# Adding and subtracting the context's halves on GpSimd instead of VectorE in a three-phase decoder kernel

## What is computed

```python
x  = _layernorm(x + attn(x))         # phase A: gated, decaying moments of sines and cosines
x  = _layernorm(x + xattn(x, ctx))   # phase B: autocorrelation attention against the context
x  = _layernorm(x + ffn(x))          # phase C: two branches of 8 experts with a running mean

# in phase B: FFT correlation of query and key along the 256 tokens
Qf = jnp.fft.rfft(Q, axis=2); Kf = jnp.fft.rfft(K, axis=2)
corr = jnp.fft.irfft(Qf * jnp.conj(Kf), n=Lloc, axis=2)
w, idx = jax.lax.top_k(corr.mean(axis=-1), top_k)      # top_k = 5
```

## Time and profile before

| | |
|---|---|
| median of 3 runs | 893.53 us (892.78 to 893.91) |
| the profiled execution: its time | 892.9 us |
| its span, first to last instruction | 891.1 us |
| TensorE busy | 823.9 us (92%) |
| VectorE busy | 754.2 us (85%) |
| ScalarE busy | 488.0 us (55%) |
| GpSimd busy | 98.0 us (11%) |
| TensorE's mean granted clock | 0.973 |

### The profile page before, as it was taken

The page is one execution under the profiler, slowest core; times in us unless marked ns, Lnnn a source line. Parts: engine busy times, 40 slices in busy tenths (PEclk is TensorE's granted clock), DMA queues, the critical chain, the costliest instruction groups (busy, mean ns, idle before and its releaser), DMA issues.

```text
span 891.1 us, 11684 instructions
## 1 busy us (share of the span) xinstructions
PE 823.9 (92%) x4040; PEld 489.4 (55%) x4040; DVE 754.2 (85%) x1351; ACT 488.0 (55%) x774; POOL 98.0 (11%) x164
## 2 busy tenths in 40 slices
PE   6886738999999999999999999999999999997996
PEld 3343515564755566565666475555656475656453
DVE  7987998899989998899989999899999996384133
ACT  4964763774558553866377545955395655202300
POOL 2021012000120012001120012001200022001000
PEclk9998968999999999999999999999999999999899
DMA  9475035232634343153622562234515251410040
GB/s 299 126 141 118 0 72 119 72 83 48 131 59 137 86 86 61 25 142 71 118 64 68 130 119 53 55 83 95 107 26 128 59 109 23 95 24 1 1 118 24
DMA packets 45968, 75.18 MB, mean 84 GB/s; under 512 B 4819, under 2 KB 28630, under 8 KB 45910
## 3 DMA queue, kind: packets, MB, share of 16 engines
q1 hardware_dynamic: 38998, 49.27, 22.3%
q0 software_dynamic: 6912, 25.17, 14.4%
HBM read 19.90 MB, written 4.19 MB: 27 GB/s over the span
## 4 chain that ended last, share of the span: by engine, by line
PE 48%; DVE 30%; DMA 8%; issue 8%; ACT 4%; SPq 1%; POOL 1%; ACTq 0%; DVEq 0%; POOLq 0%
DVE sc L2528 7%; PE ps L902 7%; DMA acc<-sq 7%; PE ps L911 7%; PE ps L867 6%; PE ps L785 5%; DVE sc L2520 4%; PE ps L709 4%; PE ps L751 3%; PE ps L927 3%; PE ps L726 3%; PE ps L769 2%; DVE zc L2458 2%; PE ps L844 2%; DVE frac L2500 2%
## 5 line engine op out<-in xcount | busy, mean ns | idle before, releaser
L2528 DVE TENSOR_TENSOR_SCAN sc<-mask,sc 128x1024 f32<-128x1024 bf16 x64 | 144.3, 2276 | 0.1
L911 PE MATMUL ps<-x2t,mv 128*128 128x512 f32 x256 | 119.0, 597 | 0.2
L902 PE MATMUL ps<-cum,mw 128*128 128x512 f32 x256 | 117.8, 596 | 0.6 <-DVE prod L2748 0.5
L927 PE MATMUL ps<-up,prod 128*128 128x256 f32 x512 | 115.3, 382 | 0.1
L927 PEld LDWEIGHTS ps<-up,prod 128*128 128x128 f32 x512 | 96.0, 190 | 17.6 <-issue 5.2
L2271 POOL DMA_DIRECT2D acc<-sq x48 | 42.3, 923 | 504.3 <-ACT sq L1570 491.5
L1570 ACT ACTIVATE sq<-sc 128x1024 f32<-128x1024 f32 x48 | 50.0, 1051 | 63.3 <-DVE sc L2528 45.0
L911 PEld LDWEIGHTS ps<-x2t,mv 128*128 128x128 f32 x256 | 47.4, 190 | 57.7 <-issue 51.1
L2520 DVE TENSOR_TENSOR sc<-sc,g 128x1024 f32<-128x1024 f32 x64 | 76.4, 1212 | 3.2 <-ACT sc L1554 3.0
L902 PEld LDWEIGHTS ps<-cum,mw 128*128 128x128 f32 x256 | 47.1, 190 | 55.0 <-issue 48.7
L2458 DVE SCALAR_TENSOR_TENSOR zc<-ps,cst,zc 128x510 f32<-128x510 f32 (+2 forms) x96 | 70.7, 744 | 6.6 <-ACT zc L1484 4.3
(11 more groups left out here) (226 smaller groups left out, 1357.5 us busy)
## 6 DMA issues: line engine op xcount, KB each, us to landing
acc<-sq POOLq DMA_DIRECT2D x48, 512.0 KB, 4.5
wb<-wT SPq DMA_DIRECT2D x64, 256.0 KB, 3.7
xt<-in_x_t_dram SPq DMA_DIRECT2D x8, 512.0 KB, 5.7
cin<-in_ctx_dram SPq DMA_DIRECT2D x8, 512.0 KB, 5.3
frac<-den SPq DMA_DIRECT2D x32, 128.0 KB, 3.7
xs_a<-in_x_dram SPq DMA_DIRECT2D x8, 512.0 KB, 5.5
out_dram<-prod SPq DMA_DIRECT2D x16, 256.0 KB, 4.0
per<-zs SPq DMA_DIRECT2D x32, 64.0 KB
```

Of the source, the lines that this page charges most:

```text
L902: last = mm(o, mw[:, t, br, c:c + P], cum[:, t, :], start=(t == 0), stop=(t == 1))
L911: last = mm(o, mv[:, t, br, c:c + P], x2t[:, t, :], start=(t == 0), stop=(t == 1))
L927: return mm(o, prod[:, j, q * P:(q + 1) * P], up[:, j, :], start=(j == 0 and q % 2 == 0), stop=stop)
L2528: V.tensor_tensor_scan(flat, mask[:, 0:2 * T], flat, 0.0, ALU.mult, ALU.add)\
```

## The change

The context's fold goes from VectorE to GpSimd as `b_split`. GpSimd's version uses three two-input operations: the difference, the doubling of the first half, and the difference of that and the first result. The other fold stays on VectorE. TensorE's transform of the context waits for GpSimd's third operation instead of VectorE's second. Every queue's list of calls is in a new order; the parts of it that the steps below speak of are shown.

```diff
-POOL_B = Steps("pool_b", each("rstd shift", range(2)))
+POOL_B = Steps("pool_b", each("fold", range(3)) + each("rstd shift", range(2)))
...
-                pe.wait_ge(*VEC_B.at(i, "fold", 1 if name == "cf" else 3))
+                pe.wait_ge(*(POOL_B.at(i, "fold", 2) if name == "cf" else VEC_B.at(i, "fold", 1)))
...
             @staged
+            def b_split(i):
+
+                pool.wait_ge(ctx_loaded, 16 * i + 16)
+                G.tensor_tensor(ch[:, 1, :, :], ch[:, 0, :, :], ch[:, 1, :, :], ALU.subtract).then_inc(*POOL_B.tick("fold", 0))
+                pool.wait_ge(*POOL_B.at(i, "fold", 0))
+                G.tensor_tensor(ch[:, 0, :, :], ch[:, 0, :, :], ch[:, 0, :, :], ALU.add).then_inc(*POOL_B.tick("fold", 1))
+                pool.wait_ge(*POOL_B.at(i, "fold", 1))
+                G.tensor_tensor(ch[:, 0, :, :], ch[:, 0, :, :], ch[:, 1, :, :], ALU.subtract).then_inc(*POOL_B.tick("fold", 2))
+
+            @staged
...
+            b_split(0)
             a_accumulate(0, 2)
...
             a_accumulate(1, 7)
+            b_split(1)
             b_rstd(0, 0)
...
             a_accumulate(2, 3)
-            a_accumulate(2, 2)
+            b_split(2)
             a_accumulate(2, 4)
...
             a_accumulate(3, 7)
+            b_split(3)
             c_rstd(1, 0)
...
             c_rstd(2, 0)
+            b_split(4)
             b_rstd(3, 0)
+            b_rstd(3, 1)
...
             a_accumulate(5, 7)
+            b_split(5)
             c_rstd(3, 0)
...
             a_accumulate(6, 2)
+            b_split(6)
             a_accumulate(6, 4)
...
+            a_accumulate(7, 2)
+            b_split(7)
+            a_accumulate(7, 4)
             a_accumulate(7, 3)
```

On VectorE the start of the list, on SyncE the loads around the first context:

```diff
             a_scores(0)
             alphas()
-            a_den(0)
             a_conv(0, 0)
...
             a_scan(0, 6)
             a_scan(0, 7)
+            a_den(0)
             biases()
             a_weight(0)
-            b_fold(0, "cf")
             a_conv(1, 0)
...
             load_weights("u")
+            load_weights("r")
             load_weights("turn")
-            load_weights("out")
             load_weights("v")
             spread_scores(0, 0)
+            load_residual(0)
+            load_x(1)
             spread_scores(0, 1)
-            load_x(1)
             load_weights("w")
+            load_weights("rest")
+            load_weights("out")
             load_weights("x")
-            load_weights("rest")
-            load_weights("r")
             load_ctx(0)
...
+            load_x(7)
+            load_residual(6)
             spread(4, 6)
             spread(4, 7)
-            spread(4, 5)
+            load_ctx(6)
             spread_factor(6, 0)
```

More of the change, by code:

```diff
@@ L118 @@
 ACT_B = Steps("act_b", each("xf cf", range(2)) + ["ot"] + SPEC + ["exp", "wt"] + NORM)
-POOL_B = Steps("pool_b", each("rstd shift", range(2)))
-VEC_B = Steps("vec_b", each("fold", range(4)) + each("ot", range(2)) + each("pr", range(3)) + ["heads", "ca", "cb0", "cb1", "cb2", "corr", "top", "negmax",
+POOL_B = Steps("pool_b", each("fold", range(3)) + each("rstd shift", range(2)))
+VEC_B = Steps("vec_b", each("fold", range(2)) + each("ot", range(2)) + each("pr", range(3)) + ["heads", "ca", "cb0", "cb1", "cb2", "corr", "top", "negmax",
                         "above", "equal", "order", "first", "also", "keep", "weight", "inv", "wn",
@@ L535, in _ @@
             spread(4, 0)
+            spread(4, 1)
+            spread(4, 3)
+            spread(4, 5)
+            spread(4, 2)
             spread(4, 4)
-            spread(4, 1)
-            spread(4, 2)
-            spread(4, 3)
+            load_x(7)
+            load_residual(6)
             spread(4, 6)
             spread(4, 7)
-            spread(4, 5)
+            load_ctx(6)
             spread_factor(6, 0)
             spread_factor(6, 1)
-            store(4, 0)
-            load_residual(6)
             spread_scores(7, 1)
             spread_scores(7, 0)
-            load_residual(7)
[L550 to L558, removed]
+            load_ctx(7)
+            spread(5, 1)
+            spread(5, 0)
+            spread(5, 4)
+            spread(5, 2)
+            spread(5, 3)
+            store(4, 0)
+            store(4, 1)
+            spread(5, 5)
+            spread(5, 6)
+            load_residual(7)
             spread(5, 7)
@@ L580, in _ @@
             spread(7, 7)
+            spread(7, 6)
+            store(6, 0)
             store(6, 1)
@@ L958, in _ @@
             a_project(0, 2)
+            fold(0)
             a_project(0, 3)
-            fold(0)
             fold(1)
@@ L1085, in _ @@
             c_hidden(1, 3)
+            b_transform(2, "cf", 0)
+            b_transform(2, "cf", 1)
+            c_logits(1)
+            b_transform(2, "xf", 0)
+            b_transform(2, "xf", 1)
+            c_turn(1)
             a_project(3, 2)
-            c_logits(1)
-            b_transform(2, "cf", 1)
             a_project(3, 3)
-            c_turn(1)
             c_running(1, 0)
+            b_spectrum(2, "qb")
+            c_weights(1)
+            b_spectrum(2, "qa")
+            c_running(1, 1)
             c_own(1, 0)
[L1093 to L1099, removed]
             c_own(1, 1)
             b_spectrum(2, "ka")
+            b_spectrum(2, "kb")
+            c_running(1, 2)
+            c_running(1, 3)
+            b_spectrum(2, "va")
+            b_spectrum(2, "vb")
             a_sums(3, 0)
@@ L1733, in _ @@
             fold(20)
+            a_gate(0, 0)
+            a_gate(0, 1)
             fold(21)
@@ L2045, in _ @@
             a_squares(5, 7)
+            a_gate(5, 0)
+            a_gate(5, 1)
+            b_back(4)
             a_guard(5)
-            b_back(4)
             a_norm(5)
```

1179 lines of the change are left out of this document (575 added, 604 removed).

## The result

The changed kernel takes 907.35 us, median of 4 runs (906.64 to 908.18), against 893.59 (892.78 to 893.91): a ratio of 1.0151, 95% interval 1.0133 to 1.0168. It is 13.8 us slower; forecast were 2.0 us, and the range ended at 904. The profiled execution has a span of 905.9 us.

What follows compares the result with a forecast made beforehand. The prediction took VectorE to bound the kernel before 161 us and TensorE after. Start +1.5 us (+3.1 - 1.0 - 0.6) and later +0.5 gave 893.5 + 2.0 = 895.5 us, range 886 to 904.

Steps and rivals of the forecast that it cites:

- What bounds the kernel: Whole kernel: VectorE bounds it before 161 us, TensorE from 161 to 812 us, with VectorE close behind at 90%.
- What is removed: VectorE's context folds, 11.0 us in all: nothing gained at chunk 0, 0.3 of the last seven, 2.9 us.
- What is added: Three GpSimd operations per chunk, 1.04 us each; they and VectorE's hold each other up, 0 to 3.1 us a split.
- VectorE goes first: Rival at the splits: VectorE takes operands first and loses nothing, 887.9 us; chance 0.30 together with a lucky order.
- Place by place: VectorE's hold per split: 3.1 us at chunk 0, 2.1 at chunks 2, 3, 6, 7, 0.5 at chunks 1, 4, 5.
- Later: +0.5: Chunks 1 to 7: savings and holds on VectorE about cancel, weighted 0.3 on the path; +0.5 us taken.
- What moves: New order of every queue: two moves priced at the start, the rest a scatter of 3.4 us without a sign.
- unlucky order: Whole kernel: new order losing 3.4 us, said to look like GpSimd's queue being late; no chance of its own.
- late queue: Rival on GpSimd: splits end late and delay accumulations and layer norms behind them, +8 us, 901.5; chance 0.18.
- two moves priced at the start: Chunk 0: denominator's scan moved behind the last scan, -1.0 us; ScalarE's last sines ahead of four copies, -0.6.
- All hidden: Rival: TensorE absorbs everything after 161 us and moved denominator and sines pay the held start, 893.5 us; chance 0.10.
- The sum: Whole kernel: start +3.1 - 1.0 - 0.6 = +1.5 us, later +0.5, together +2.0 us, 895.5.

Runs made afterwards that it cites:

- no_fold: Kernel before with the context's fold left out, that part of the computation missing: 894.1 us against 893.0, ratio 1.0012.
- order_only: New order of all queues, context's fold kept on VectorE in its two operations, none on GpSimd: 898.3 us, ratio 1.0056 to the kernel before.
- no_split: Changed kernel with its three 128x512 GpSimd operations per chunk replaced by 128x2 operations on a scratch tile, context not added and subtracted: 898.6 us.
- move_write: Kernel before's order, context's fold left out, three GpSimd fills per chunk at the changed kernel's places in GpSimd's queue: 900.4 us.

## Why the prediction was wrong

*What bounds the kernel* held: TensorE from 161 us on, VectorE before. *What is removed* failed in its share. Of the last seven folds 0.3 were to be gained; no_fold measured a gain of none. The chain shows one path that ended last. Beside it TensorE's own queue was as long (idle 6.5 of 651 us), so shortening the one moved nothing. Chunk 0's fold was rightly counted at zero.

*What is added* was near in size: 1.04 us forecast for an operation, 1.04 measured undisturbed for the one and 1.27 for the two that read both halves. For these two the estimate of some 1.3 us from the Trainium skill (GPSIMD Engine Reference, section Performance versus the Vector engine) was the nearer one. That the engines hold each other was right as well; *VectorE goes first* is refuted by operations of 1.75 instead of 0.68 us.

*Place by place* came near in its sum, 3.1 + 4 x 2.1 + 3 x 0.5 = 13.0 us against 15.1, in part by luck: it was 4.5 us too low at chunks 1, 3, 5 and 6 and 2.3 too high at the others. Chunks 1 and 5 were put down as quiet and held 3.0 and 1.3 us, by the products of phase B and the scan of the denominator, while chunk 4, put down likewise, held nothing.

The step that failed first is the balance made from it, "Later: +0.5": savings and holds of chunks 1 to 7 were set against each other and both weighted with 0.3. They don't weigh the same. Savings counted 0; holds counted 8.2 to 8.8 of 15.1 us in the new order, more than half, and about all of 20.2 us in the old one, with what the clock added. TensorE's waits for VectorE, 2.0 us before and 6.9 and 13.8 with the two holds, show the path. Why the two weigh so differently is my reading: VectorE is 90% busy in the steady part, and an operation taken away lies mostly where TensorE sets the pace, while a held one delays the products and scans on which TensorE's next sums wait.

*What moves* is the second step that failed. A scatter of 3.4 us without a sign stood for the order; it measured +5.3 us (order_only), and the sum had nothing for it. The nearest forecast was the unlucky order of 3.4 us named under *late queue*; that rival's own mechanism was the wrong one: not the splits came late, but one accumulation behind another, and the lower clock behind TensorE's wait for it was in no term. The two moves priced at the start, -1.6 together, agree with no_split's first mark, 1.35 us ahead of before, as far as one execution tells. *All hidden* held for the removal alone.

*The sum*: forecast +2.0. Measured: +5.3 for the order, 0 for the removal, +8.2 to +8.8 for the operations (no_split to the change), against 13.8 in all. By the marks of the profiled execution the start came to +0.7 where +1.5 was told, and all the rest lies behind it, where +0.5 was told.

Of what was named to be seen, VectorE's operations at a split were longer by 0.2 to 1.9 us, where 0.5 to 1.0 was told, and the last scan of chunk 0 ended 1.5 us later (60.9 instead of 59.4), as told. TensorE's share from 161 us on fell to 97.8% where 98 to 99% was told, and chunk 7's stage took 104 us, which was named as upsetting everything: those were the signs of the loss. The layer norm of chunk 5's split, which began 0.1 us behind it, looked like *late queue* and wasn't, as it waited for VectorE.

## What to carry to other kernels

Work moved from VectorE to GpSimd is paid by what VectorE reads at that moment, not by GpSimd's idle time: put it beside VectorE operations with an operand in PSUM, where the same 3.7 us splits cost nothing that could be measured, and not beside those with two SBUF tensors, where eight of them cost 8 to 23 us. Where two engines are both near their bound, a saving on the one off the pace can be worth nothing and a delay on it half of its length or all of it; weigh them apart. In an in-order queue, look for a call that stands behind a later one: a single accumulation was 3.8 us. And look at the granted clock behind a new wait: 2.7 us of waiting were followed by matmuls that took 1.5 us longer.

## What the hardware showed that was not expected

Fills on GpSimd, which read nothing, left VectorE's two-input operations alone (1.23 and 0.68 us) and held single-input ones of SBUF to SBUF: 1.15 instead of 0.28 us, 2.40 instead of 0.34. The Trainium skill (SBUF — State Buffer, section Who interferes with whom) has both halves: two SBUF inputs meet GpSimd's reads alone, while operations such as a tensor with a scalar can use both ports and then meet any GpSimd access. The runs agree, as far as these clamps and this scaling show it. Which engine goes first can't be read off the starts of the records, as the prediction had done: the scaling's begins 0.57 us ahead of the fill that held it, and at chunk 6's split a moment that begins 0.48 us ahead of GpSimd's first operation takes 3.13 us instead of 1.22. Both times GpSimd was issuing accumulations just then, but in the kernel before the same scaling beside the same two accumulations took 0.34 us. Records on GpSimd are rough, and I leave it open.

Two engines that hold each other do so in turn, operation by operation: GpSimd's three took 1.75, 1.90 and 2.12 us, VectorE's three 0.8 to 1.0 us more each, and neither got two in a row there.

With the folds left out, TensorE's granted clock from 75 to 88 us was 0.57 and 0.50 instead of 0.79 and 1.00 (1.00 instead of 0.79 in the eight microseconds before), and the start's gain of 0.6 us was gone. In the steady part the clock fell to 0.50 behind single waits: behind 2.7 us in the changed kernel, 2.4 in order_only, 1.6 in move_write. The stage means, which round to 1.00, don't show it; rows of a few microseconds behind a wait do.
